# A fused transformer stage on one core: softmax sums moved ahead of a gating product, other orders in the first and last steps, a split pair of refill parts

## What is computed

```python
x = x + 0.5 * ffn(layernorm(x))
x = x + attn(layernorm(x))
x = x + 0.5 * ffn(layernorm(x))
```

## Time and profile before

| what | value |
|---|---|
| median of three runs | 2123.13 us (2120.92 to 2124.13) |
| the profiled execution, its own time | 2123.92 us |
| its span | 2122.2 us |
| TensorE, matmuls | 2083.8 us busy, 98% |
| TensorE, weight loads | 1910.3 us, 90% |
| VectorE | 1357.8 us, 64% |
| ScalarE | 961.8 us, 45% |
| GpSimd | 494.1 us, 23% |
| granted clock of TensorE, mean | 0.997 |

### The profile page before, as it was taken

How to read it: one execution, slowest core, us unless ns; L and a number is a source line. 1 busy time by engine, 2 the same in 40 slices (tenths; PEclk the granted TensorE clock), 3 DMA queues, 4 the chain that set the end, 5 groups by cost and what they waited for, 6 DMA issues and landing times.

```text
span 2122.2 us, 37639 instructions
## 1 busy us (share of the span) xinstructions
PE 2083.8 (98%) x13844; PEld 1910.3 (90%) x13844; DVE 1357.8 (64%) x3108; ACT 961.8 (45%) x1910; POOL 494.1 (23%) x433
## 2 busy tenths in 40 slices
PE   8999999999999999999999999999999999999999
PEld 7888899999998788888887878888999999988888
DVE  7666556666665577878887986665466666633333
ACT  3333335555553465555565552333455555522222
POOL 3423211121212233222334443322021211200000
PEclk9999999999999999999999999999999999999999
DMA  9231225554436344444445442231244444531010
GB/s 279 100 112 59 75 64 132 134 142 110 105 91 191 88 112 110 110 110 95 117 108 140 120 108 79 74 95 48 80 104 113 101 99 104 127 116 60 30 61 21
DMA packets 295976, 218.70 MB, mean 103 GB/s; under 512 B 69241, under 2 KB 276525, under 8 KB 295792
## 3 DMA queue, kind: packets, MB, share of 16 engines
q1 hardware_dynamic: 278128, 194.92, 32.6%
q0 software_dynamic: 17664, 21.38, 5.8%
HBM read 129.48 MB, written 93.23 MB: 105 GB/s over the span
## 4 chain that ended last, share of the span: by engine, by line
PE 85%; DVE 7%; issue 3%; ACT 1%; DMA 1%; SPq 1%; POOL 1%; DVEq 0%; ACTq 0%; POOLq 0%
PE gate_up_p L347 27%; PE quad L347 25%; PE out_p L385 22%; PE misc L385 4%; PE quad L570 2%; DVE p_s L1169 1%; PE misc L539 1%; PE quad L571 1%; PE misc L411 1%; DMA stage<-in_L_ffn_rd 1%; DVE h_s L1034 1%; PE misc L422 1%; PE misc L403 1%; PE misc L420 1%; DVE den_a L1193 1%
## 5 line engine op out<-in xcount | busy, mean ns | idle before, releaser
L347 PE MATMUL gate_up_p<-zh,w 128*128 128x512 f32 (+2 forms) x2368 | 703.3, 359 | 4.1 <-DVE h_s L1034 3.5
L721 ACT CAST hh<-h_s 128x512 fp32r<-128x512 f32 (+2 forms) x511 | 276.2, 541 | 681.6 <-DVE h_s L1034 663.5
L347 PE MATMUL quad<-zh,w 128*128 128x512 f32 (+2 forms) x1728 | 481.7, 346 | 0.0
L347 PEld LDWEIGHTS gate_up_p<-zh,w 128*128 128x128 f32 x2368 | 429.5, 188 | 52.4 <-DVE h_s L1034 5.1
L385 PE MATMUL out_p<-w,hh 128*128 128x256 f32 x2808 | 458.7, 282 | 5.8 <-DVE hl L1118 2.7
L385 PEld LDWEIGHTS out_p<-w,hh 128*128 128x128 f32 x2808 | 403.7, 189 | 29.2 <-DVE hl L1118 5.6
L347 PE MATMUL gate_up_p<-zl,w 128*128 128x512 f32 (+2 forms) x1184 | 421.4, 356 | 0.0
L1034 DVE TENSOR_TENSOR h_s<-gate_up_p,sg_s 128x512 f32<-128x512 f32 (+2 forms) x296 | 178.5, 603 | 254.4 <-PE gate_up_p L347 239.7
L1050 DVE TENSOR_TENSOR hl<-h_s,hh 128x512 fp32r<-128x512 f32 (+2 forms) x431 | 247.1, 573 | 136.6 <-ACT hh L721 121.2
L347 PEld LDWEIGHTS quad<-zh,w 128*128 128x128 f32 x1728 | 308.5, 188 | 24.6
L347 PE MATMUL quad<-zl,w 128*128 128x512 f32 (+2 forms) x864 | 295.4, 342 | 0.0
(11 more groups left out here) (189 smaller groups left out, 2526.8 us busy)
## 6 DMA issues: line engine op xcount, KB each, us to landing
stage<-in_L_ffn_rg SPq DMA_DIRECT2D x128, 128.0 KB, 2.8
stage<-in_L_ffn_ru SPq DMA_DIRECT2D x128, 128.0 KB, 3.0
stage<-in_L_ffn_rd SPq DMA_DIRECT2D x128, 128.0 KB, 3.1
heads_d<-qkh SPq DMA_DIRECT2D x128, 128.0 KB
q_t<-heads_d SPq DMA_DIRECT2D x32, 384.0 KB, 4.6
k_t<-heads_d SPq DMA_DIRECT2D x64, 192.0 KB, 4.8
slots_d<-empty SPq DMA_DIRECT2D x16, 662.5 KB, 7.0
zh_d<-zh SPq DMA_DIRECT2D x16, 512.0 KB, 3.2
```

The source lines that it names most:

```text
L347: last = pe.matmul(dst, a, b, start=(k == 0), stop=(k == 3 * n - 1))
L721: nc.scalar.copy(hh[:, n % 2, 0:ncol], h_s[:, n % 2, 0:ncol]).then_inc(sm["hh_done"], 1)
```

## The change

Lines of the changed kernel are 6 to 20 higher than before. With names as above:

- **The sums.** In steps with `probs` and c not 0, VectorE forms `den_a` and `rden` right behind `qke`, ahead of `h_s` of n; before, they stood behind `qkl`, ahead of the mask. Where c = 0 they stay.
- **First steps.** `heads_first` is now true where there is a `z` and either c = 0 or no `out`: that adds steps 5, 6 and 7, in which q, k and v now go ahead of `h_s` of n on VectorE (with `hl` of n behind the mask) and `qkh` ahead of `hh` of n on ScalarE. In steps 0 and 4, which have c = 0 and no `z`, ScalarE now rounds `hh` of n ahead of the SiLU of n + 1. In step 6 (`keys` without `probs`), TensorE forms the scores behind `up` of n + 1, and VectorE `h_s` of n + 1 ahead of the mask.
- **Last steps.** In steps 37, 38 and 39 (`out` without `z`, `drained`), VectorE forms `h_s` of n right behind the projection's addition, ahead of the preparation and `pl`. In step 38 TensorE does the probability transposes ahead of the early down product.
- **Refill.** GpSimd forms the second low part of a refill step in the next step, behind `qkr` and the small preparation and ahead of the subtraction; the first stays where it was.

The helper that tells a refill step's first piece:

```diff
+        def refill(s):
+            if s < 0:
+                return -1
+            f, phase, b, c = fused_chunk(s)
+            return c - 2 if phase == "s1" and b == NB - 1 else c + NCH - 2 if phase == "s0" and b == 0 else -1
```

TensorE's `fused_step`:

```diff
                 if out is not None:
                     y_transpose(out)
+                if probs is not None and keys is None:
+                    prob_transposes(probs, z, uses)
                 if early_down:
                     down_of(*chunk_before(f, phase, b, c))
-                if probs is not None:
+                if probs is not None and keys is not None:
                     prob_transposes(probs, z, uses)
...
-                if keys is not None:
+                if keys is not None and probs is not None:
                     scores(keys, z, out)
                 up(n + 1, b % 2, c + 1, buf, SB)
+                if keys is not None and probs is None:
+                    scores(keys, z, out)
```

ScalarE's:

```diff
-                if c:
+                heads_first = z is not None and (c == 0 or out is None)
+                if not heads_first:
                     h_high(n, SB)
                 silu(n + 1, SB)
                 if z is not None:
                     heads_high(z)
-                if not c:
+                if heads_first:
                     h_high(n, SB)
```

VectorE's:

```diff
+                drained = z is None and out is not None
+                if drained:
+                    h_product(n, SB)
                 if s:
                     others(s - 1, 0)
                     others(s - 1, 1)
...
-                if z is None or c:
+                if probs is not None and c:
+                    row_sums(probs)
+                    inverse_sums(probs)
+                heads_first = z is not None and (c == 0 or out is None)
+                if not heads_first and not drained:
                     h_product(n, SB)
-                if z is not None and c:
+                if z is not None and not heads_first:
                     qk_normal(z)
                     values_low(z)
...
-                if c:
+                if not heads_first:
                     fused_low(n)
                 if z is not None:
                     heads_low(z)
-                if probs is not None:
+                if probs is not None and not c:
                     row_sums(probs)
                     inverse_sums(probs)
+                if keys is not None and probs is None:
+                    h_product(n + 1, SB)
                 if keys is not None:
                     masked(keys)
-                if not c:
+                if heads_first:
                     fused_low(n)
                 if keys is not None:
                     highest(keys)
-                h_product(n + 1, SB)
+                if keys is None or probs is not None:
+                    h_product(n + 1, SB)
```

GpSimd's:

```diff
                 prep_fused(s)
+                if 0 <= refill(s - 1) < NCH:
+                    piece_low(refill(s - 1) + 1)
                 if keys is not None:
...
-                if 0 <= refill < NCH:
-                    piece_low(refill)
-                    piece_low(refill + 1)
+                if 0 <= refill(s) < NCH:
+                    piece_low(refill(s))
```

More of the change, by code:

```diff
@@ L776, in fused_step @@
                 pf, pb = prep_block(f, phase, b)
-                refill = c - 2 if phase == "s1" and b == NB - 1 else c + NCH - 2 if phase == "s0" and b == 0 else -1
                 if out is not None:
@@ L799, in fused_step @@
                     heads_high(z)
-                if not c:
+                if heads_first:
                     h_high(n, SB)
                 prep(pf, pb, c)
-                if 0 <= refill < NCH:
-                    piece_high(1, 0, refill)
+                if 0 <= refill(s) < NCH:
+                    piece_high(1, 0, refill(s))
                 if keys is not None:
@@ L815, in fused_step @@
                 prep(pf, pb, c + 1)
-                if 0 <= refill < NCH:
-                    piece_high(1, 0, refill + 1)
+                if 0 <= refill(s) < NCH:
+                    piece_high(1, 0, refill(s) + 1)
             def fused():
```

## The result

| | median us | runs | lowest to highest |
|---|---|---|---|
| before, in the same comparison | 2123.13 | 5 | 2120.92 to 2126.61 |
| changed | 2112.07 | 5 | 2109.86 to 2113.96 |

What follows compares the result with a forecast made beforehand. TensorE, nine tenths busy or more in every slice but the first, was taken as the bound, gains coming only where it stands still. Terms summed to -9.8 from 2123.92, so 2114.1, placed at 2113.5 us; range 2109.5 to 2119.

Steps and rivals of the forecast that it cites:

- Sums, -7.95 for the plain steps: 15 plain steps between 760 and 1080 us: each loses its whole 0.53 us stall of `values` behind the mask.
- the rival that it is not: Slot ahead of `h_s` not free: the sums push `h_s`, `vv` and scores; 2122 us, chance 0.09.
- First steps, -1.32 together: Steps 0 and 4 -0.85, steps 5 and 6 together +0.6, step 7 -1.07 us, from waits removed or exchanged.
- The exchange in step 6: Step 6: the 1.76 us wait for `k_t` goes; the down product waits for mask and `hl`, 1.16 + 0.7 us.
- the 0.6 us that sticks out in steps 5 and 6: Steps 5 and 6: later `h_s` is mostly hidden by the second gate product; about 0.6 us delays the second `up`.
- refill at 0: Steps 29 to 33: moving the second low part gains 0 us, between -1.05 and +1.37.
- the sums at +0.4: Steps 33 to 35, VectorE behind: the sums push `qk`, `vv` and scores, costing 0.4 us (0 to 1.8).
- The port rule: VectorE instructions with two SBUF inputs and GpSimd reads take turns; in step 31 `hl` would be held, about 1 us worse.
- Last steps, -0.9: Steps 37 to 39: waits for `h_s` go but mostly move to `pl` and `hl`; -0.9 us (0 to -3.2).
- The clock, a rival at 0.20: Half-clock stretches: without the long one at 1129.6, 2110 us; with one or two more, 2115 to 2117; chance 0.20.

Runs made afterwards that it cites:

- sums_alone: The kernel before with only the sums moved ahead of `h_s` in steps with `probs` and c not 0: 2117.62 us against 2123.91.
- best: The changed kernel with sums early in c = 0 steps too and further reordering in steps 5, 6 and 37 to 39: 2103.38 us, ratio to before 0.9903.
- refill_alone: The kernel before with only the refill's second low part formed a step later: 2120.34 us against 2123.91, ratio 0.9971.
- last_alone: The kernel before with only the last steps' orders (37 to 39): 2126.35 us against 2123.91, ratio 1.0007.
- end_low: The changed kernel with other orders in the last steps alone, sums of steps 37 and 38 behind the projection's addition: 2106.63 us.
- sums_all: The changed kernel with the sums moved ahead of `h_s` in the c = 0 steps too: 2110.75 us, ratio to before 0.9928.

## Why the prediction was right and wrong

- **Sums, -7.95 for the plain steps:** right in mechanism, place and count. Measured -7.25 in the trace of the change and -7.3 in sums_alone. The mis-sized step is the mask's end: "ends at 870.40, just ahead of 870.46" took its duration of 1.16 us from a row behind `rden`, and left out the 0.06 us from its end to `values`. Behind `qkl` it takes 1.23 us, and 0.05 us of each stall stays; why the instruction ahead matters, no run shows. The slot was free, as said; the rival that it is not falls.
- **First steps, -1.32 together:** -1.2 in the trace of the change, of which step 7's mask is the sums' part; -0.8 alone. The exchange in step 6 (`hl` behind the mask for `k_t`) and the 0.6 us that sticks out in steps 5 and 6 (0.70 measured) came as worked out.
- **Steps 28 to 36, refill at 0 and the sums at +0.4:** -0.7 in the trace, 0.2 +- 0.4 for the refill alone at full clock. The sums' +0.4 did not come: from one first `values` to the next, step 33 to 34 is 0.23 longer (18.95 against 18.72), 34 to 35 is 0.36 shorter (17.82 against 18.18) and 35 to 36 is the same. What the port rule of the Trainium skill ("SBUF — State Buffer", section "SBUF: two separate sides") made likely did happen, though to `azn` and not to step 31's `hl`: 1.24 us beside the moved part against 0.41. The rule as the prediction puts it names two SBUF inputs. The trace agrees with it in `hl` at 1165.99 and in best at 714.82 (2.28 us against 0.68); `azn`, which reads one tensor and two columns, was slow in the same way.
- **Last steps, -0.9:** right as an order (1.0 alone at full clock), with the waits for `pl` and `hl` in the places named. Not seen were the longer wait for the mask in step 37 (1.28 instead of 0.6) and the clock: the profiled stage came out 1.2 longer than before, 1.7 of it from the longer half-clock stretch. That the sums move in steps 37 and 38 too had no term.
- **The clock, a rival at 0.20, and the refill's 0:** this is the step that failed. The prediction took the half-clock stretches of one profiled execution as the kernel's own, and asked which of them would move; for the refill it counted waits alone, 0 between -1.05 and +1.37. The 78 runs show that the loss to the clock differs from run to run and is 12.2 us on the mean for the kernel before, where its first profile shows 13.6 us at half clock in the fused stage, 6.8 lost. And an order shifts that mean: the refill's part alone lowers it (12.2 to 6.4), so that refill_alone is 3.6 us under before in the median, outside those bounds, with nothing gained at full clock; the last steps' part raises it (to 15.4). For the whole change it falls from 12.2 to 9.7, worth 1.9 +- 1.1 us. At full clock the change is worth 9.2 of the 9.8 that the sum gives; with the 1.9 that makes 11.1, which is by construction the difference of the means (2124.9 over 78 runs, 2113.7 over 12). So the terms were 0.6 too high together, and the clock's share, put at nothing, more than made up for it. That this share is why the time came out below the forecast fits the numbers, but 1.9 +- 1.1 is not clear of noise by itself.

The agreement of the profiled pair (10.0 against 9.8) was partly luck: 2.1 us of it lie outside the fused stage.

Open is what in the refill brings the stretches: GpSimd's second part ahead of `half_s`, the later row halves or the work that then meets; no run separated them. So is where a run of before at a clock of 0.990 loses its time.

## What to carry to other kernels

Work that no one needs yet belongs into a slot where its engine waits for something else: the sums cost nothing there, in plain steps and in c = 0 steps. Moving a wait ahead of another does not end it: look up what the instruction that is now later releases, and mend the whole chain (last_alone gained 1.0 at full clock, end_low 3.7 more). With effects under 1%, read the granted clock of many runs beside the times before believing a difference of medians, since an order can change how often the clock falls.

## What the runs showed of the hardware

- TensorE's granted clock differs between executions of one program: 0.989 to 0.998 in the mean over 78 runs of the kernel before, with times from 2133.15 to 2117.78, and 0.996 to 0.998 over 12 runs of refill_alone. A us lost to it costs 0.78 us of time. In the fused stage, stretches at the 1.2 GHz level lay only where TensorE waits or works on small products (first steps, refill and the steps behind it, last steps), never in the plain steps of any of the 14 profiles.
- The same mask on VectorE takes 1.16 us right behind `rden` (128x16) and 1.21 to 1.23 behind `qkl`, `hl` or `h_s` (128x512), also where its inputs had been there for 0.79 and 2.47 us: 1.16 in the c = 0 steps of the changed kernel, 1.23 in the same steps of sums_all, in which only the sums ahead of it were moved.
- VectorE's `azn`, which reads only one tensor of 128x256 from SBUF beside two columns, took 1.24 us beside a low part of the refill on GpSimd (a subtraction of two SBUF tensors of 128x768), and 0.41 in plain steps.
